# Group scores as the largest of ten pair sums, with new orders of work on all engines

## The chip, the cores and the metric

The kernel runs on one core of a Trainium2 chip. The metric is the device time of one execution in microseconds (us). Five engines work side by side, each through its own list of instructions in order, and wait for each other by semaphores: PE (TensorE, matrix products), DVE (VectorE), ACT (ScalarE), POOL (GpSimd) and SP (SyncE, which only starts DMAs here).

## The reference

The input is x, 2 batches x 1024 tokens x 128 channels in float32. A block of attention comes first, then a mixture of experts, each with a layer norm before and after and added to x:

```python
x = x + _layernorm(attn(_layernorm(x), W_basis, W_v, b_v, W_o, b_o))
x = x + _layernorm(ffn(_layernorm(x), gate_w, gate_bias, Wg, Wu, Wd, Sg, Su, Sd))

# attn: latent = x @ W_basis.T (R = 64); scores = latent @ latent.T / 8, causal softmax
# ffn: 64 experts of 88 hidden units, 2 shared ones; all experts are computed, rw weighs them
scores = sigmoid(x @ gate_w.T); choice = scores + gate_bias
group_scores = sum(top_k(choice.reshape(T, 8, 8), 2)[0], axis=-1)
_, gidx = top_k(group_scores, 4)          # 4 of 8 groups stay
_, idx = top_k(where(in_group, choice, 0), 8)
rw = 2.5 * scores[idx] / (sum(scores[idx]) + 1e-20)
routed = einsum('eth,te->th', expert_out, rw); out = routed + shared
```

The change touches one line of this, the sum of the two largest of each group of eight.

## The kernel before

The 2048 tokens are 16 tiles of 128, in four quads (q = 0 to 3) of four tiles; quads 0 and 1 are the first batch. The hidden units of the experts are cut into 11 rounds of 4 sets; a set is 128 hidden units, 8 of each of 16 experts. A step is one set (or shared expert part) with one quad of 512 tokens: gate and up products (six matmuls of 512 columns, since each float32 factor is split into a high and a low part and three products are taken), a SiLU on ACT, two products on DVE, the split of the hidden tile into high (ACT) and low (POOL), and the down product (three matmuls) into a PSUM bank that gathers the output of a quad.

Everything up to the end of round 0 is written out, step by step, by four lists of stages, `PE_ORDER`, `ACT_ORDER`, `DVE_ORDER` and `POOL_ORDER`; every engine runs its list in order and every stage holds its own waits. Rounds 1 to 9 follow in loops (`Fori`) that the change leaves alone. Round 10 and the output are written out again in `PE_TAIL`, `ACT_TAIL`, `DVE_TAIL` and `POOL_TAIL`.

A stage is a letter and a quad, with a tile number behind it for A, C, N and T. What the letters do:

- A: score rows of a tile (PE), row maximum (DVE L895), exponent (ACT L702). T: the exponents transposed by PE and copied by ACT (L712). C: weighing the values (PE L1258), squares and copy on ACT (L690, L693). D: the inverse root for the norm behind attention (POOL L539). U: adding attention to x (DVE L908). V, Q, P, S: values, latent, transposed norm and statistics of x.
- X: statistics of the new x on DVE (L864, L867), inverse root and shift on POOL (L523 to L530). Y: its norm on ACT (L672). E: transposed by PE (L1268), kept as x2_t and x_hi by ACT (L719, L720), x_lo by POOL (L512).
- F: logits (PE L1277), tanh (ACT L726), the sigmoid from it (DVE L925), the bias (POOL L587). H: group scores (DVE L935 to L945). J: choice of groups (DVE L953 to L960) and masking (POOL L596). I: choice of experts (DVE). O: their scores picked (DVE L976). M: the sum of weights (DVE L981 to L984) and the routes (POOL L575). G: the routes transposed (PE L1286), high part (ACT L734), low part (DVE L919). N: the routes spread over hidden units, two sets a stage (PE L1301, ACT L740).
- Z: gate and up of step q, on ACT the SiLU, on DVE the products (L1008, L1018, or L1080 for shared parts). Steps Z0 and Z1 are the shared parts of quad 0, Z2 to Z5 its four sets; Z6 to Z17 belong to quads 1 and 2, Z18 to Z23 to quad 3. W: hidden tile into high (ACT L768) and low (POOL L547); on PE, W of k is the down product of step k - 2. R: an expert set's weights split into high (ACT L748) and low (POOL L555). L: the same for the shared ones. B, K: small preparations.
- In the tail Z, W and R are as above, D is a down product, O the copy of a finished quad, T its centering on PE (L1457), S statistics, Y the inverse root on POOL, N the output.

Step Z with an odd number uses PSUM banks 2 and 3, which N uses too, so that Z3 waits for ACT's copies of N01. Route stages share bank 1 with F. H waits for the biased scores and sits in DVE's list like any other stage. These lines set two of the waits:

```python
if routed:
    pe.wait_ge(s_wlo, c + 1)          # first_gate_up: low weights of set c, stage R on POOL
pe.wait_ge(s_xlo, q + 1)
if s % 2 == 1:
    banks23_free(at)
...
def spread_route(q, h, at):           # stage N
    pe.wait_ge(s_rt, q + 1)           # low part of the routes, stage G on DVE
```

`link` gives an instruction an increment and waits for it, where the next pass reads what it wrote.

Of the kernel before, what the change touches and what calls it, by code (L numbers as in the profile page):

```python
# [51 lines left out]
def build(nc, x, w_basis_t, w_v, b_v, w_o_t, b_o, gate_w_t, gate_bias, w_experts, w_shared_up,  # L52
# [21 lines left out]
    with ExitStack() as ctx:  # L74
# [312 lines left out]
        def unit_bank(u):  # L387
# [1115 lines left out]
```

## Time and profile before

| | us |
|---|---|
| three runs | 480.24, 482.01, 482.15 |
| median | 482.01 |
| the profiled execution | 481.66 |
| its span, first to last instruction | 479.7 |
| mean granted clock of PE in the span | 0.992 |

The profile is of one execution. A page sums it up; behind it are views that group instructions by line, that list them in order of time (the timeline, with the idle time of the engine before each and what ended it), and that give the busy time of each engine in a window. All times are from the start of the span. The granted clock is 1.00 at 2.4 GHz and 0.50 at 1.2 GHz.

### The profile page before, as it was taken

The numbers are of one execution on the slowest core, as the hardware profiler recorded it, in microseconds if no ns is written. First come the engines' busy times: TensorE is split into PE (matmuls) and PEld (weight loads), VectorE is DVE, ScalarE is ACT, GpSimd is POOL, SyncE is SP. The second block draws the span as 40 slices with busy tenths as digits, with TensorE's granted clock in tenths as the row PEclk, the third lists the DMA queues.
The fourth block names the chain that finished last, engine by engine and source line by source line (L and its number), as shares of the span: only waits on it lengthen the run. The fifth ranks groups of instructions, "written<-read, shape, count | busy, mean of one in ns | idle before, by whom it ended". The sixth has DMA issues, their size and how long they took to land.

```text
span 479.7 us, 8058 instructions
## 1 busy us (share of the span) xinstructions
PE 454.6 (95%) x2152; PEld 370.0 (77%) x2152; DVE 326.3 (68%) x710; ACT 286.2 (60%) x573; POOL 335.5 (70%) x318
## 2 busy tenths in 40 slices
PE   6899876889999999999999999999999999999995
PEld 5788764667678888888888888888888888888884
DVE  5667879677566666666666666666666666666777
ACT  2688874765655655565555655555565555556554
POOL 6581845848577777767777777768776776778684
PEclk9999988999999999999999999999999999999999
DMA  7000100000011010100001010100001010100002
GB/s 182 21 3 1 33 2 8 27 1 0 1 34 35 16 34 16 34 16 20 29 16 33 16 33 16 33 16 20 30 16 33 16 33 16 32 1 0 0 24 66
DMA packets 12856, 11.58 MB, mean 24 GB/s; under 512 B 2549, under 2 KB 12837, under 8 KB 12837
## 3 DMA queue, kind: packets, MB, share of 16 engines
q1 hardware_dynamic: 11973, 11.02, 8.1%
q10 hardware_dynamic: 864, 0.33, 0.3%
q8 instruction: 9, 0.15, 0.1%
q14 instruction: 10, 0.08, 0.1%
HBM read 10.30 MB, written 1.05 MB: 24 GB/s over the span
## 4 chain that ended last, share of the span: by engine, by line
PE 84%; DVE 5%; POOL 4%; ACT 2%; issue 2%; DMA 1%; ACTq 0%; DVEq 0%; POOLq 0%
PE ps L1306 26%; PE ps L1308 26%; PE ps L1307 25%; PE ps L1258 2%; PE ps L1246 1%; PE ps L1457 1%; DVE neg_max L895 1%; PE ps L1301 1%; POOL xn L565 1%; POOL rstd L524 1%; DMA bv_sb<-in_b_v 1%; PE ps L1198 1%; DVE hid L1080 1%; POOL x_lo L512 1%; POOL w_lo L555 0%
## 5 line engine op out<-in xcount | busy, mean ns | idle before, releaser
L547 POOL TENSOR_TENSOR lat_hi<-hid,lat_hl 128x512 fp32r<-128x512 f32 (+1 forms) x187 | 240.5, 1288 | 96.7 <-ACT lat_hl L768 95.9
L754 ACT ACTIVATE ps<-ps 128x512 f32<-128x512 f32 (+1 forms) x180 | 103.0, 573 | 132.6 <-PE ps L1308 132.4
L1008 DVE TENSOR_TENSOR up_w<-ps,route_w 128x512 f32<-128x512 f32 (+1 forms) x180 | 122.1, 678 | 83.0 <-PE ps L1308 82.5
L1018 DVE TENSOR_TENSOR hid<-ps,up_w 128x512 f32<-128x512 f32 (+1 forms) x180 | 122.4, 680 | 36.5 <-DVE up_w L1008 28.3
L1306 PE MATMUL ps<-x_hi,w_hi 128*128 128x512 f32 (+1 forms) x360 | 141.0, 392 | 1.5 <-POOL w_lo L555 1.1
L1308 PE MATMUL ps<-x_hi,w_lo 128*128 128x512 f32 (+1 forms) x360 | 140.4, 390 | 0.0
L1307 PE MATMUL ps<-x_lo,w_hi 128*128 128x512 f32 (+1 forms) x360 | 140.1, 389 | 0.0
L768 ACT CAST lat_hl<-hid 128x512 fp32r<-128x512 f32 (+1 forms) x188 | 113.6, 605 | 17.8 <-DVE hid L1018 17.1
L1306 PEld LDWEIGHTS ps<-x_hi,w_hi 128*128 128x128 f32 x360 | 68.0, 189 | 18.1 <-POOL w_lo L555 1.5
L1308 PEld LDWEIGHTS ps<-x_hi,w_lo 128*128 128x128 f32 x360 | 67.9, 189 | 14.9
L1307 PEld LDWEIGHTS ps<-x_lo,w_hi 128*128 128x128 f32 x360 | 67.9, 189 | 14.5
L1306 PE MATMUL ps<-lat_hl,w_hi 128*128 128x512 f32 (+1 forms) x180 | 71.1, 395 | 0.0
L1308 PE MATMUL ps<-lat_hl,w_lo 128*128 128x512 f32 (+1 forms) x180 | 69.7, 387 | 0.0
L1307 PE MATMUL ps<-lat_hi,w_hi 128*128 128x512 f32 (+1 forms) x180 | 69.2, 385 | 0.0
L555 POOL TENSOR_TENSOR w_lo<-w_raw,w_hi 128x384 fp32r<-128x384 f32 x44 | 44.8, 1018 | 2.5 <-ACT w_hi L748 2.5
L1308 PEld LDWEIGHTS ps<-lat_hl,w_lo 128*128 128x128 f32 x180 | 33.7, 187 | 8.1
L1306 PEld LDWEIGHTS ps<-lat_hl,w_hi 128*128 128x128 f32 x180 | 33.8, 188 | 7.8 <-issue 0.7
L1307 PEld LDWEIGHTS ps<-lat_hi,w_hi 128*128 128x128 f32 x180 | 33.8, 188 | 7.3
L748 ACT CAST w_hi<-w_raw 128x384 fp32r<-128x384 f32 x44 | 22.8, 518 | 4.2 <-PE ps L1308 4.2
L1258 PE MATMUL ps<-vals,exp_t 128*128 128x129 f32 x144 | 19.5, 288 | 0.3 <-ACT att L693 0.2
L1258 PEld LDWEIGHTS ps<-vals,exp_t 128*128 128x128 f32 x144 | 18.3, 202 | 1.6 <-issue 1.5
L895 DVE TENSOR_REDUCE neg_max<-ps 128x1 f32<-128x128 f32 (+7 forms) x16 | 12.0, 753 | 9.6 <-PE ps L1228 9.5
(140 smaller groups left out, 363.2 us busy)
## 6 DMA issues: line engine op xcount, KB each, us to landing
w_raw<-in_w_experts SPq DMA_DIRECT2D x44, 192.0 KB, 2.3
x_sb<-in_x SPq DMA_DIRECT2D x3, 256.0 KB, 4.8
out<-x_sb SPq DMA_DIRECT2D x3, 256.0 KB, 2.3
x_sb<-in_x ACTq DMA_DIRECT2D x2, 64.0 KB, 2.3
x_sb<-in_x SPq DMA_DIRECT2D x2, 64.0 KB, 2.1
out<-x_sb SPq DMA_DIRECT2D x1, 128.0 KB, 1.8
out<-x_sb SPq DMA_DIRECT2D x2, 64.0 KB, 1.6
sh_raw<-in_w_shared_up SPq DMA_DIRECT2D x1, 88.0 KB
```

Source lines behind the costliest of these rows:

```text
L547: g.tensor_tensor(hid_lo[:, k % DEEP, 0:w], hid[:, k % 2, 0:w], hid_hi[:, k % DEEP, 0:w], ALU.subtract).then_inc(s_hlo, 1)
L555: g.tensor_tensor(w_lo[:, c, :], w_raw[:, c, :], w_hi[:, c, :], ALU.subtract).then_inc(s_wlo, 1)
L748: a.copy(w_hi[:, c, :], w_raw[:, c, :]).then_inc(s_whi, 1)
L754: a.activation(bank, bank, ACT.Silu).then_inc(s_gated, 1)
L768: a.copy(hid_hi[:, k % DEEP, 0:w], hid[:, k % 2, 0:w]).then_inc(s_hhi, 1)
L895: v.tensor_reduce(neg_max[:, k:k + 1], rows.rearrange("p a b -> p (a b)")[:, 0:width], AX.X, ALU.max, negate=True).then_inc(s_max, 1)
L1008: v.tensor_tensor(up_w[:, k % 2, 0:w], ps[:, gate_bank(k) + 1, 0:w], route_w[:, group, 512 * q + lo:512 * q + lo + w], ALU.mult).then_inc( ...
L1018: v.tensor_tensor(hid[:, k % 2, 0:w], ps[:, gate_bank(k), 0:w], up_w[:, k % 2, 0:w], ALU.mult).then_inc(s_hid, 1)
L1258: mm = t_.matmul(ps[:, 7, 256 * (r % 2):256 * (r % 2) + C + 1], exp_t[:, r % 2, j, :], vals[:, (q // QPB) * TPB + j, 0:C + 1], start=(j == 0),
L1306: t_.matmul(out_, hi, mhi, start=start, stop=False)
L1307: t_.matmul(out_, hi, mlo, start=False, stop=False)
L1308: return t_.matmul(out_, lo, mhi, start=False, stop=stop)
```

## The change

H on DVE takes seven passes instead of eleven. Before, it kept the largest and second largest of halves, quarters and eighths of a group in turn. Now it takes the larger and smaller of element k and k + 4 (four high and four low values) and forms ten sums: each high with its own low, and the six pairs of two high ones. The sum of the two largest of the group is the largest of these ten. The ten sums lie in a tile `pair_sum`, and one reduction over it gives the score.

The eight lists have the same stages as before in other orders. The first part of the diff declares the tiles; the lists are shown whole.

```diff
--- before.py
+++ after.py
@@ -131,9 +131,9 @@
 
         scores = sb("scores", [P, 2, 4, E])
         choice = sb("choice", [P, 2, 4, E])
-        big = [sb(f"big{n}", [P, 4 * GROUPS, 4 >> n]) for n in range(3)]
-        small = [sb(f"small{n}", [P, 4 * GROUPS, 4 >> n]) for n in range(3)]
-        low_big = sb("low_big", [P, 4 * GROUPS, 2])
+        high = sb("high", [P, 4 * GROUPS, 4])
+        low = sb("low", [P, 4 * GROUPS, 4])
+        pair_sum = sb("pair_sum", [P, 4 * GROUPS, 10])
         group_score = sb("group_score", [P, 4, GROUPS])
         group_find = sb("group_find", [P, 4, 8])
         group_left = sb("group_left", [P, 4, GROUPS])
@@ -260,33 +260,33 @@
             return [stage(name) for name in names.split()]
 
         PE_ORDER = stages(
-            "P0 Q0 K0 V0 P1 A00 A01 Q1 T00 T02 A02 A03 C00 C01 T04 T06 A10 A11 C02 C03 T10 A12 "
-            "T11 V1 T12 P2 A13 T13 Q2 C10 W0 C11 P3 T14 V2 T15 A20 Q3 T16 T17 C12 A21 C13 A22 "
-            "E0 V3 F0 T20 A23 T22 A30 T24 A31 C20 T26 C21 A32 W1 T30 T31 C22 C23 T32 T33 C30 "
-            "E1 A33 T34 F1 T35 C31 T36 T37 G0 Z0 C32 N00 E2 C33 Z1 F2 N01 G1 Z2 Z3 Z4 W2 W3 E3 "
-            "Z5 W4 Z6 N10 F3 W5 N11 G2 Z7 W6 W7 N20 Z8 Z9 W8 N21 Z10 Z11 W9 Z12 Z13 W10 W11 "
-            "W12 Z14 Z15 W13 G3 W14 Z16 N30 W15 W16 Z17 Z18 N31 W17 W18 Z19 Z20 W19 Z21 W20 "
+            "P0 Q0 K0 V0 A00 P1 A01 A02 Q1 T00 T02 A03 C00 C01 T04 T06 A10 C02 C03 A11 P2 V1 "
+            "T10 A12 T11 A13 W0 T12 Q2 T13 C10 C11 P3 T14 V2 T15 Q3 A20 T16 A21 T17 C12 C13 E0 "
+            "A22 A23 T20 F0 A30 T22 T24 V3 A31 T26 C20 C21 A32 C22 T30 T31 C23 T32 T33 C30 A33 "
+            "E1 T34 F1 T35 W1 C31 G0 T36 T37 Z0 C32 N00 C33 Z1 E2 F2 Z2 N01 G1 Z3 W2 Z4 W3 Z5 "
+            "E3 W4 Z6 N10 F3 N11 G2 W5 Z7 W6 W7 N20 Z8 Z9 W8 N21 Z10 Z11 W9 W10 Z12 W11 Z13 "
+            "W12 W13 Z14 Z15 G3 W14 Z16 N30 W15 W16 Z17 Z18 N31 W17 W18 Z19 Z20 W19 Z21 W20 "
             "Z22 W21 W22 Z23 "
         )
         ACT_ORDER = stages(
-            "P0 Q0 K0 P1 A00 A01 Q1 T00 T02 A02 A03 T04 C01 T06 A10 C03 T10 A11 T11 T12 P2 T13 "
-            "Q2 A12 C11 P3 A13 T14 T15 A20 L0 T16 T17 Q3 Y0 C13 A21 E0 F0 A22 T20 A23 T22 L1 "
-            "R0 A30 T24 T26 C21 R1 A31 T30 T31 C23 Y1 T32 T33 A32 E1 A33 T34 F1 T35 C31 T36 R2 "
-            "T37 G0 Z0 Y2 N00 E2 C33 Z1 R3 F2 W0 G1 N01 W1 Z2 W2 Z3 Z4 Y3 W3 E3 Z5 W4 W5 Z6 "
-            "N10 F3 N11 G2 W6 Z7 N20 W7 Z8 Z9 W8 N21 W9 Z10 Z11 Z12 W10 W11 Z13 W12 Z14 W13 "
-            "Z15 G3 W14 W15 Z16 N30 Z17 W16 W17 Z18 N31 Z19 W18 W19 Z20 W20 Z21 W21 Z22 R4 Z23 "
-            "W22 R5 "
+            "P0 Q0 K0 P1 A00 A01 Q1 T00 T02 A02 A03 T04 C01 T06 A10 C03 L0 A11 P2 T10 T11 T12 "
+            "T13 A12 Q2 C11 P3 A13 T14 T15 Q3 A20 T16 T17 Y0 C13 E0 A21 F0 A22 T20 T22 A23 A30 "
+            "T24 C21 R0 R1 T26 A31 T30 T31 C23 L1 T32 Y1 T33 A32 E1 T34 F1 A33 T35 C31 T36 G0 "
+            "R2 T37 Z0 N00 Y2 C33 Z1 E2 R3 F2 G1 W0 N01 W1 Z2 W2 Z3 Z4 Y3 W3 Z5 W4 E3 Z6 W5 "
+            "N10 F3 N11 W6 G2 Z7 N20 W7 Z8 Z9 W8 N21 Z10 W9 W10 Z11 Z12 W11 W12 Z13 W13 Z14 "
+            "Z15 G3 W14 Z16 N30 W15 W16 Z17 Z18 N31 W17 W18 Z19 W19 Z20 Z21 W20 W21 Z22 R4 W22 "
+            "Z23 R5 "
         )
         DVE_ORDER = stages(
-            "S0 B0 P0 S1 S2 B1 Q0 A00 A01 K0 V0 A02 A03 Q1 S3 A10 A11 A12 V1 U0 X0 Q2 A13 V2 "
-            "A20 A21 Q3 A22 U1 V3 F0 A23 A30 H0 X1 A31 J0 A32 I0 O0 M0 A33 U2 X2 F1 H1 G0 J1 "
-            "Z0 I1 O1 Z1 U3 F2 M1 H2 J2 X3 Z2 I2 G1 Z3 O2 Z4 Z5 M2 F3 Z6 G2 Z7 H3 Z8 Z9 J3 Z10 "
-            "Z11 I3 Z12 Z13 O3 M3 Z14 Z15 G3 Z16 Z17 Z18 Z19 Z20 Z21 Z22 Z23 "
+            "S0 B0 P0 S1 S2 B1 Q0 A00 A01 A02 K0 V0 A03 Q1 S3 A10 A11 A12 V1 U0 A13 Q2 X0 V2 "
+            "A20 A21 Q3 A22 A23 U1 F0 A30 X1 V3 H0 A31 A32 J0 I0 O0 M0 A33 U2 F1 X2 H1 G0 J1 "
+            "Z0 I1 O1 Z1 U3 F2 M1 H2 J2 X3 Z2 I2 Z3 G1 Z4 O2 Z5 M2 Z6 F3 G2 Z7 H3 Z8 Z9 J3 Z10 "
+            "I3 Z11 O3 Z12 M3 Z13 Z14 Z15 G3 Z16 Z17 Z18 Z19 Z20 Z21 Z22 Z23 "
         )
         POOL_ORDER = stages(
-            "S0 S1 P1 S2 P2 D0 S3 P3 B0 X0 D1 F0 X1 J0 L0 E0 D2 L1 R0 M0 R1 E1 F1 X2 J1 E2 D3 "
-            "F2 M1 J2 W0 R2 X3 W1 R3 W2 W3 W4 M2 F3 W5 W6 W7 W8 W9 J3 W10 W11 W12 M3 W13 W14 "
-            "W15 E3 W16 W17 W18 W19 W20 W21 R4 W22 R5 "
+            "S0 S1 P1 B0 S2 P2 D0 S3 P3 X0 D1 F0 X1 L0 J0 D2 E0 R0 M0 F1 R1 X2 E1 L1 J1 D3 E2 "
+            "F2 M1 W0 R2 J2 W1 X3 R3 W2 W3 W4 M2 F3 W5 W6 E3 W7 W8 J3 W9 W10 W11 W12 M3 W13 "
+            "W14 W15 W16 W17 W18 W19 W20 W21 R4 W22 R5 "
         )
         ROWS = [(q, r) for q in range(QUADS) for r in range(4)]
         TURNS = [(q, 2 * r + h) for q, r in ROWS for h in range(1 + (4 * (q % QPB) + r) // 4)]
@@ -388,22 +388,22 @@
             return (6, 7, 0, 7, 1)[u]
 
         PE_TAIL = stages(
-            "Z0 D0 Z1 D1 D2 Z2 D3 Z3 Z4 D4 Z5 D5 Z6 Z7 D6 D7 Z8 T0 Z9 D8 D9 Z10 D10 Z11 Z12 T1 "
-            "D11 Z13 D12 Z14 Z15 D13 D14 D15 Z16 Z17 D16 T2 D17 D18 Z18 Z19 T3 D19 D20 D21 D22 "
+            "Z0 D0 Z1 D1 D2 Z2 D3 Z3 Z4 D4 D5 Z5 D6 Z6 Z7 D7 Z8 T0 Z9 D8 Z10 D9 D10 Z11 Z12 T1 "
+            "D11 Z13 D12 Z14 D13 Z15 D14 Z16 D15 Z17 T2 D16 D17 D18 Z18 T3 Z19 D19 D20 D21 D22 "
             "T4 "
         )
         ACT_TAIL = stages(
-            "R2 W0 Z0 W1 Z1 R3 W2 Z2 W3 Z3 Z4 W4 W5 Z5 Z6 W6 W7 Z7 O0 Z8 W8 W9 Z9 Z10 W10 O1 "
-            "W11 Z11 Z12 W12 W13 Z13 Z14 Z15 W14 W15 W16 Z16 O2 Z17 W17 W18 Z18 Z19 O3 W19 W20 "
+            "W0 Z0 R2 Z1 W1 R3 W2 Z2 Z3 W3 Z4 W4 W5 Z5 Z6 W6 O0 Z7 W7 Z8 W8 W9 Z9 W10 Z10 O1 "
+            "W11 Z11 Z12 W12 W13 Z13 Z14 W14 Z15 O2 Z16 W15 W16 Z17 O3 W17 W18 Z18 Z19 W19 W20 "
             "Y4 P0 "
         )
         DVE_TAIL = stages(
-            "Z0 Z1 Z2 Z3 Z4 Z5 Z6 Z7 Z8 S0 Z9 Z10 Z11 Z12 S1 Z13 N0 Z14 Z15 N1 Z16 Z17 S2 Z18 "
+            "Z0 Z1 Z2 Z3 Z4 Z5 Z6 Z7 Z8 S0 Z9 Z10 N0 Z11 Z12 S1 Z13 Z14 Z15 N1 Z16 Z17 S2 Z18 "
             "Z19 W20 S3 O4 N2 S4 N3 N4 "
         )
         POOL_TAIL = stages(
-            "W0 R2 W1 R3 W2 W3 W4 W5 W6 W7 W8 Y0 W9 W10 W11 W12 W13 Y1 W14 W15 W16 W17 W18 Y2 "
-            "W19 Y3 "
+            "W0 R2 W1 R3 W2 W3 W4 W5 W6 W7 W8 W9 Y0 W10 W11 W12 W13 Y1 W14 W15 W16 W17 W18 W19 "
+            "Y2 Y3 "
         )
 
         def acc_bank(q):
@@ -932,18 +932,15 @@
                     dve.wait_ge(s_gin, q)
 
                 grp = choice[:, k].rearrange("p t (g k) -> p (t g) k", k=GE)
-                tt(big[0][:], grp[:, :, 0:4], grp[:, :, 4:8], ALU.max)
-                link(tt(small[0][:], grp[:, :, 0:4], grp[:, :, 4:8], ALU.min))
-                for n in range(2):
-                    w = 2 >> n
-                    b0, b1 = big[n][:, :, 0:w], big[n][:, :, w:2 * w]
-                    tt(big[n + 1][:], b0, b1, ALU.max)
-                    tt(low_big[:, :, 0:w], b0, b1, ALU.min)
-                    link(tt(small[n + 1][:], small[n][:, :, 0:w], small[n][:, :, w:2 * w],
-                            ALU.max))
-                    link(tt(small[n + 1][:], small[n + 1][:], low_big[:, :, 0:w], ALU.max))
-                link(tt(group_score[:, :, :].rearrange("p t g -> p (t g)"), big[2][:, :, 0],
-                        small[2][:, :, 0], ALU.add))
+                tt(high[:], grp[:, :, 0:4], grp[:, :, 4:8], ALU.max)
+                link(tt(low[:], grp[:, :, 0:4], grp[:, :, 4:8], ALU.min))
+                tt(pair_sum[:, :, 0:4], high[:], low[:], ALU.add)
+                tt(pair_sum[:, :, 4:7], high[:, :, 0:3], high[:, :, 1:4], ALU.add)
+                tt(pair_sum[:, :, 7:9], high[:, :, 0:2], high[:, :, 2:4], ALU.add)
+                link(tt(pair_sum[:, :, 9:10], high[:, :, 0:1], high[:, :, 3:4], ALU.add))
+                link(v.tensor_reduce(group_score[:, :, :].rearrange("p t g -> p (t g)"),
+                                     pair_sum[:], AX.X, ALU.max))
+
             def choose_groups(q):
 
                 if q:
```

## Rows read from the trace of the kernel before

**Rows 1.** Busy time of each engine over the whole span, from the page

```profile
PE 454.6 (95%) x2152; PEld 370.0 (77%) x2152; DVE 326.3 (68%) x710; ACT 286.2 (60%) x573; POOL 335.5 (70%) x318
```

**Rows 2.** Windows: length, busy PE, PEld, DVE, ACT, POOL; granted clock, DMA

```profile
178.00:435.00 257.00, 257.00 (x1114) 208.66 (x1113) 171.13 (x248) 149.50 (x279) 190.57 (x155) 1.00 0.08 23
...
31.00:60.00 29.00, 26.63 (x205) 23.75 (x204) 21.01 (x71) 25.16 (x72) 16.47 (x23) 1.00 0.05 15
60.00:88.30 28.30, 19.75 (x93) 15.69 (x92) 23.07 (x112) 17.40 (x38) 15.86 (x21) 0.88 0.05 13
88.30:135.00 46.70, 43.92 (x188) 32.31 (x187) 30.30 (x80) 29.07 (x54) 30.23 (x26) 1.00 0.01 2
66.00:70.00 4.00, 3.71 (x21) 3.58 (x21) 3.85 (x23) 2.33 (x5) 1.84 (x2) 0.58 0.00 2
76.00:80.00 4.00, 3.85 (x12) 3.27 (x13) 3.65 (x28) 2.57 (x5) 0.66 (x2) 0.57 0.00 0
```

**Rows 3.** Timeline, PE after its waits: start us, us, what, [idle before, releaser]

```profile
13.77 0.63 PE L1162 MATMUL ps<-ident,xn 128*128 128x128 f32 x4 [1.02 <-POOL xn L565]
...
53.51 0.66 PE L1268 MATMUL ps<-ident,xn 128*128 128x128 f32 x4 [0.84 <-ACT exp_t L712]
...
65.44 0.73 PE L1301 MATMUL ps<-route_t,sel 128*128 128x512 f32 x2 [2.58 <-issue]
...
76.14 1.05 PE L1286 MATMUL ps<-ident,route 128*128 128x128 f32 x4 [2.71 <-POOL route L575]
```

**Rows 4.** Timeline of DVE from 60 to 65 us

```profile
60.14 0.87 DVE L864 BATCH_NORM_STATS2 stats<-x_sb 128x6 f32<-128x128 f32 x4
...
61.34 0.26 DVE L925 TENSOR_SCALAR scores<-scores 128x256 f32<-128x256 f32 x1
62.44 0.29 DVE L935 TENSOR_TENSOR big<-choice 128x128 f32<-128x128 f32 x1 [0.84 <-POOL choice L587]
62.65 0.28 DVE L936 TENSOR_TENSOR small<-choice 128x128 f32<-128x128 f32 x1
...
64.41 0.19 DVE L945 TENSOR_TENSOR group_score<-big,small 128x32 f32<-128x32 f32 x1
64.64 0.69 DVE L919 TENSOR_TENSOR route_t<-ps,route_t 64x512 fp32r<-64x512 f32 x1
```

**Rows 5.** DVE reductions by form, 0 to 130 us: busy us, mean ns, idle

```profile
L981 DVE TENSOR_REDUCE wsum<-left 128x4 f32<-128x256 f32 x4 | 1.7, 414 | 0.1
...
L895 DVE TENSOR_REDUCE neg_max<-ps 128x1 f32<-128x384 f32 x2 | 1.1, 558 | 1.1 <-PE ps L1228 1.1
```

**Rows 6.** Timelines of DVE and POOL: the same passes alone and beside POOL

```profile
41.21 1.14 DVE L908 SCALAR_TENSOR_TENSOR x_sb<-att,rstd,x_sb 128x128 f32<-128x128 f32 x4 [1.14 <-POOL rstd L539]
...
56.34 3.77 DVE L908 SCALAR_TENSOR_TENSOR x_sb<-att,rstd,x_sb 128x128 f32<-128x128 f32 x4
...
74.96 1.04 POOL L575 TENSOR_TENSOR route<-left,winv 128x512 f32<-128x512 f32 x1 [0.32 <-DVE winv L984]
...
74.99 1.16 DVE L936 TENSOR_TENSOR small<-choice 128x128 f32<-128x128 f32 x1
```

**Rows 7.** Costs on POOL (page, then timeline) and on ACT (timeline)

```profile
L547 POOL TENSOR_TENSOR lat_hi<-hid,lat_hl 128x512 fp32r<-128x512 f32 (+1 forms) x187 | 240.5, 1288 | 96.7 <-ACT lat_hl L768 95.9
...
L555 POOL TENSOR_TENSOR w_lo<-w_raw,w_hi 128x384 fp32r<-128x384 f32 x44 | 44.8, 1018 | 2.5 <-ACT w_hi L748 2.5
...
62.49 0.33 POOL L523 TENSOR_SCALAR var_e<-mv 128x4 f32<-128x4 f32 x1
...
64.37 0.20 POOL L530 TENSOR_TENSOR shift<-var_e,rstd 128x4 f32<-128x4 f32 x1
...
77.71 1.08 ACT L740 COPY route_w<-ps 128x512 f32<-128x512 f32 x2
```

**Rows 8.** Timelines of PE and POOL near the end

```profile
471.92 0.71 PE L1457 MATMUL ps<-center,y_t 128*128 128x128 f32 x4 [0.61 <-ACT y_t L843]
...
471.05 1.04 POOL L524 TENSOR_TENSOR rstd<-var_e,minus_half 128x4 f32<-128x4 f32 x1
```

## The prediction

> **What bounds the kernel now.** I read the page first, then windows by stage, then the timelines of the engines. TensorE is busy for 95% of the span [rows 1], but the share is an average over three stages. In the loop over the rounds it has no idle time: 257 of 257 us, 1114 matmuls, so 0.231 us each [rows 2]. Nothing in the diff touches that loop, and no faster route can shorten it. From 31 to 60 us (the attention of the second half) PE is idle for 29.0 - 26.6 = 2.4 us, from 60 to 88.3 us (routing beside the first experts) for 28.3 - 19.75 = 8.55 us, and from 88.3 to 135 us for 2.8 us [rows 2]. This idle time, some 14 us, is all that a new order can win on the way to the loop. To it comes a clock effect in the middle stage: the granted clock means 0.58 from 66 to 70 us and 0.57 from 76 to 80, which is the lower level, 1.2 GHz, for most of both. Each fall stands right behind a long pause of PE, of 2.58 and of 2.71 us [rows 3]. Their cost is 3.71 x 0.42 + 3.85 x 0.43 = 3.2 us [rows 2].
>
> The two pauses name the chain. The first, ahead of N00 at 65.44 us, is put down to issue; but N00 needs the low part of the routes, which DVE finishes at 64.64 + 0.69 = 65.33 us [rows 4]. DVE had it behind X2 (60.14), F1 (61.34), a wait of 0.84 for the biased scores from POOL, and H1, the group scoring itself, 62.44 to 64.64 [rows 4]. The second pause, ahead of G1 at 76.14, ends when POOL has written the routes of quad 1 [rows 3]. So the bound from 60 to 88 us is a loop of DVE, POOL and ACT in turn, with PE at its end.
>
> **The change, part by part.** *The scoring.* Before, H takes 2.20 us from its first pass to the next stage. An unlinked 128x128 pass holds DVE for 0.21 us, the last linked pass, of 32 elements, for 0.23 [rows 4]. The new passes are 128 and 128 elements (0.21, and 0.32 with its link), then 128, 96, 64 and 32 (0.21, 0.18, 0.14, 0.23), then a reduction of 320 elements. No row shows that reduction; between 256 elements at 414 ns and 384 at 558 [rows 5] it is 0.41 to 0.56, and I take 0.48, with a link 0.52. The sum is 1.81, so 0.4 us less for each of four H: 1.6 us of DVE. Only H1 and H2 lie where DVE is waited for. If runs of ten elements were slow and the reduction took twice that, H would be as long as before and the forecast 0.8 us worse.
>
> *The start.* A00 goes ahead of P1 and fills the 1.02 us wait of PE for xn at 13.77 [rows 3] with three short matmuls: -0.35 us.
>
> *The rows, 31 to 60 us.* A33 moves ahead of E1, where PE waited 0.84 us for exp_t behind Y1 on ACT [rows 3]; A22 and A23 move ahead of T20 and F0. R0, R1 and L1 on ACT now stand directly ahead of copies that PE needs (about 0.5 us each for R), so part comes back. Walked queue by queue, small waits of 0.2 to 0.4 us stay at C30, E1 and T34 and the 2.4 us become 1.4: -1.0. From both ends: all 2.4 go, or 1 is added.
>
> *N00.* On DVE F1 goes ahead of X2, on POOL F1 ahead of R1 and E1. POOL now stands in F1 until DVE has passed U2. Queued behind it are R1, X2, E1, L1 and J1; DVE waits for X2's result through ACT, and J1. But this leaves U2 alone on DVE: its four passes took 3.77 us at 56.34 beside a busy POOL and 1.14 alone at 41.21 [rows 6]. F1 comes at about 55.5, POOL adds the bias during X2 (the 0.84 wait is covered), H1 runs from about 57 and G0 ends near 60, while PE reaches N00 only near 61: the pause of 2.58 goes. What is late next is ACT: its queue (Z0's gate with the table load, N00's copies, Y2, C33's square, Z1, then E2's copy) delivers x2_t some 1.2 us after PE wants it for F2. The exchange of E2 and C33 on PE hides only E2.
>
> *G1, Z3, Z5.* Z2 now stands ahead of N01 and G1, so six matmuls (1.39 us) cover the route chain (F2, M1 on DVE, M1 on POOL); I get 0.85 us of wait at G1 for the 2.71 before. The cover is spent: behind G1 comes Z3, which needs both copies of N01, and on ACT these stand behind G1's copy and W0. That is four copies of 0.54 [rows 7], 2.2 us of new wait. Then Z5 needs R3, on POOL behind W0, R2, J2, W1, X3: after G1 two copies on ACT (1.1), then 1.29 + 1.02 + 0.65 + 1.29 + 2.1 (62.49 to 64.57) + 1.02 = 7.35 [rows 7], 8.45 in all; PE has G1, the wait, Z3, W2, Z4, W3 = 0.4 + 2.2 + 18 x 0.231 = 6.75, so it waits 1.7 to 1.9. With 0.15 at Z4 the stage holds 1.2 + 0.85 + 2.2 + 0.15 + 1.9 = 6.3 us instead of 8.55: -2.25.
>
> *The clock.* Two falls followed pauses of 2.6 and 2.7 us; the pauses now are 2.2 and 1.9 at most. I keep one fall of the two: -1.6, with 0 and -3.2 as ends.
>
> *DVE beside POOL.* H1 now runs while POOL works through R1 and X2. A 0.28 us pass of H2 took 1.16 us when POOL's route pass had begun 0.03 us before it [rows 6], so +0.9 for one such collision; I take +0.6, since G0 ends about 1 us before PE wants it. The Trainium skill (SBUF — State Buffer, "Who interferes with whom") says that a VectorE instruction with two SBUF inputs and a GpSimd instruction that reads SBUF lock each other out, and that tensor_reduce never does. By that rule, with which the 1.16 us agrees, six of the seven new passes can still be blocked, one for as long as a POOL instruction lasts.
>
> *88.3 to 135 us.* The waits at Z7, N20 and N21 shrink with a shorter H3 and an earlier G2; I3 and O3 now stand ahead of Z11 and Z12 on DVE, which gives some back: 2.8 becomes 2.1, -0.7 (ends -2 and +1).
>
> *The tail.* T3 moves ahead of Z19 and O3 on ACT ahead of W17 and W18. That removes the 0.61 us wait at 471.92 [rows 8] but holds back Z19, on whose hidden tile D22 waits; Y2 on POOL (1.04 us at 471.05 for its second step [rows 8]) goes behind W19 and delays N2. Sum +0.3, ends -0.4 and +0.8.
>
> The sum: -0.35 - 1.0 - 2.25 - 1.6 + 0.6 - 0.7 + 0.3 = -5.0 us. The profiled execution took 481.66 us (span 479.7), so 476.7; it lies 0.35 below the median of the three runs, 482.01, so I say 477.0.
>
> **The rivals.** *More is won, 474.* If the clock does not fall at all (-1.6) and the waits at Z3 and Z5 are half of my walk (about -2), 477.0 becomes 473.4 to 474. For it: PE is never idle as long as before either fall. Against it: the pauses stand close together.
>
> *The wait moves, 480.3.* The chain behind G1 ends no earlier because something before it slips, and the freed pauses come back at F2, Z3 and Z5: 2 us more of waits than my 6.3 and both falls of the clock (+1.6) leave 477.0 + 3.6 = 480.6, and 480.3 with the start better filled. For it: the new cover order has Z3 and Z5 exposed. Against it: N00's pause goes by two independent reasons.
>
> *Slower, 484.5.* DVE and POOL now start their two-input passes at the same time more often. If H1, O1 and H2 are stretched as U2 was, by (3.77 - 1.14) / 4 = 0.66 us a pass [rows 6], six passes each in H1 and H2 and one in O1 add 8.6 us to the chain of G1 and Z5, less some 1 us of slack at N00. That puts 477.0 at 484.5. It decides from about 5 us of stretch on, where the gain is gone. Against it: POOL's queue has gaps of its own there, and three of the four H before ran at full speed. The Trainium skill's rule above is what would cause it.
>
> *The change does not do what it says,* H as long as before: 477.8, inside the first range.
>
> **How the numbers follow.** Forecast 477.0 (its own range 474.5 to 479.5) 0.57; more is won 0.18; the wait moves 0.18; slower 0.07. The range for 8 in 10 takes in most of the second and third case and stops short of the fourth: 473.3 to 481.2. A measurement of this kernel can tell about 0.5%, 2.4 us, from no change, so faster means under 479.6: 0.57 x 0.98 + 0.18 = 0.74; slower over 484.4: 0.05; the same: 0.21.
>
> **What would show it.** Right: the loop's window still without idle time; no pause of over 1 us ahead of N00; the four passes of U2 near 1.1 us; H at 1.8 us; PE ready for Z3 before ACT has N01's copies; at most one stretch at the lower clock. Wrong: idle time from 31 to 60 us above 2.4 us, so that ACT bounds the rows; passes of H1 or H2 stretched beside POOL; a pause at Z5 of over 3 us; or waits inside the loop, which would say that the order leaves a mark there.

## The result, and the profile after

The changed kernel took 476.53 us (median of four runs, 475.69 to 477.60) beside 481.22 for four runs of the kernel before, a ratio of 0.9886 with the interval 0.9864 to 0.9909. Over the later comparisons the kernel before had medians of 482.01 to 482.16, so the gain is 4.7 to 5.5 us. The forecast was 477.0. The profiled execution of the changed kernel is its slowest of the four: 477.60 us, span 475.6. Behind H, line numbers are three lower than before.

The busy time of the engines, from the page, beside [rows 1]; then the windows of [rows 2], with a window at the start and one around the low clock:

```profile
PE 455.8 (96%) x2152; PEld 370.5 (78%) x2152; DVE 325.5 (68%) x694; ACT 286.0 (60%) x573; POOL 335.9 (71%) x318
```

```profile
135.00:435.00 300.00, 300.00 (x1299) 243.47 (x1299) 199.86 (x289) 175.01 (x327) 224.07 (x183) 1.00 0.08 23
31.00:60.00 29.00, 27.73 (x214) 24.84 (x214) 22.29 (x87) 25.46 (x72) 12.91 (x18) 1.00 0.03 8
60.00:88.30 28.30, 22.47 (x114) 17.60 (x112) 25.19 (x100) 20.28 (x45) 20.30 (x26) 0.88 0.08 22
88.30:135.00 46.70, 44.80 (x191) 33.17 (x190) 30.05 (x73) 29.18 (x55) 30.37 (x26) 1.00 0.02 5
9.00:18.00 9.00, 8.27 (x31) 6.18 (x32) 4.84 (x18) 2.89 (x7) 8.37 (x12) 0.62 0.36 103
74.00:81.00 7.00, 4.78 (x11) 3.80 (x12) 6.67 (x38) 4.08 (x8) 5.61 (x7) 0.51 0.11 30
```

The loop is as before: 300 us without idle time, 0.231 us a matmul. Idle time fell from 2.37 to 1.27 us from 31 to 60 us, from 8.55 to 5.83 from 60 to 88.3, and from 2.78 to 1.90 up to 135. The matmul counts of the windows rose because more of the work is done by then. Around the middle one stretch at the low clock is left, 74 to 81 us, but it is as long as the two of before together: the mean from 60 to 88.3 us is 0.88 in both kernels.

The row of 9 to 18 us is new: clock 0.62, where the same window of the kernel before has 1.00:

```profile
9.00:18.00 9.00, 6.85 (x38) 5.05 (x39) 5.86 (x19) 4.46 (x12) 8.62 (x12) 1.00 0.36 103
```

The fall begins at about 9 us, ahead of anything that the change moves. Stage V2 begins at 33.28 us instead of 31.84, so this execution lost 1.44 us by then, and the changed kernel profiled again below (e9_after_again) did nearly the same. Seven of the fourteen executions profiled in this study have a clock of 0.62 to 0.81 in that window, two of them with the old start (e1_passes, e3_f1first), so it is not peculiar to the change; in five of the seven the fall comes at about 14 us. Stages are compared from V2 on.

PE after its waits, beside [rows 3] and [rows 8]:

```profile
68.55 1.08 PE L1274 MATMUL ps<-gw_sb,x_t 128*128 128x64 f32 x8 [1.38 <-ACT x_t L719]
...
73.23 0.63 PE L1283 MATMUL ps<-ident,route 128*128 128x128 f32 x4 [1.70 <-POOL route L575]
...
76.22 0.77 PE L1303 MATMUL ps<-x_hi,w_hi 128*128 128x512 f32 x1 [2.37 <-ACT route_w L740]
...
97.49 0.70 PE L1298 MATMUL ps<-route_t,sel 128*128 128x512 f32 x2 [1.05 <-DVE hid L1077]
...
468.87 0.39 PE L1303 MATMUL ps<-lat_hl,w_hi 128*128 128x256 f32 x1 [0.49 <-POOL lat_hi L547]
```

The pause ahead of N00 is gone (it begins at 63.12), and on DVE two stages of the chain to it, U2 and G0, are short and early:

```profile
57.02 1.13 DVE L908 SCALAR_TENSOR_TENSOR x_sb<-att,rstd,x_sb 128x128 f32<-128x128 f32 x4
...
61.78 0.69 DVE L919 TENSOR_TENSOR route_t<-ps,route_t 64x512 fp32r<-64x512 f32 x1
```

On PE no wait over 0.3 us stands ahead of Z4 or Z5. F2, G1 and Z3 wait 1.38, 1.70 and 2.37. At N21 the wait is what it was (1.06 before). In the tail the 0.61 ahead of T3 is gone and 0.49 ahead of D19 has come.

The gain by stages, from the starts of PE's stages in the traces (us; e4_front is the changed kernel with the old tail, below):

| from, to | before | after | e4_front |
|---|---|---|---|
| V2 to N00 | 33.60 | 29.84 | 29.84 |
| N00 to G1 | 10.70 | 10.11 | 10.12 |
| G1 to N21 | 25.04 | 24.26 | 23.99 |
| N21 to T4 | 373.37 | 372.96 | 372.61 |
| V2 to T4 | 442.71 | 437.17 | 436.56 |

Two thirds of the 5.54 us lie ahead of N00. One trace of a kernel is not exact to the last digit: from F2 to F3 the changed kernel took 19.22 us here and 18.83 when it was profiled again.

### The profile page after: what moved, and what is told of

It reads as the page before. It is cut to its first block, busy times and chain, and to the rows that moved or that the text cites. A ratio compares the mean times of both kernels' runs of the same rounds, so it can differ in the third digit from the quotient of the medians.

```text
span 475.6 us, 8043 instructions
## 1 busy us (share of the span) xinstructions
PE 455.8 (96%) x2152; PEld 370.5 (78%) x2152; DVE 325.5 (68%) x694; ACT 286.0 (60%) x573; POOL 335.9 (71%) x318
## 3 DMA queue, kind: packets, MB, share of 16 engines
HBM read 10.30 MB, written 1.05 MB: 24 GB/s over the span
## 4 chain that ended last, share of the span: by engine, by line
PE 89%; ACT 5%; DVE 2%; issue 2%; DMA 1%; ACTq 0%; POOL 0%; DVEq 0%
PE ps L1303 27%; PE ps L1305 26%; PE ps L1304 26%; PE ps L1255 2%; PE ps L1243 1%; PE ps L1203 1%; PE ps L1274 1%; PE ps L1298 1%; PE ps L1195 1%; PE ps L1223 1%; PE ps L1224 1%; PE ps L1454 1%; DMA bv_sb<-in_b_v 1%; ACT xn L672 1%; ACT exp_t L712 1%
## 5 line engine op out<-in xcount | busy, mean ns | idle before, releaser
L1255 PE MATMUL ps<-vals,exp_t 128*128 128x129 f32 x144 | 18.3, 278 | 0.6 <-ACT att L693 0.4
L1255 PEld LDWEIGHTS ps<-vals,exp_t 128*128 128x128 f32 x144 | 17.1, 191 | 1.4 <-issue 1.2
```

The source lines that it names most:

```text
L1255: mm = t_.matmul(ps[:, 7, 256 * (r % 2):256 * (r % 2) + C + 1], exp_t[:, r % 2, j, :], vals[:, (q // QPB) * TPB + j, 0:C + 1], start=(j == 0),
```

## The experiments

Ratios are to the kernel before, with their 95% intervals. All kernels compute the whole of the reference.

### One half of the change at a time

**e1_passes**: the seven passes, every list as before. **e2_orders**: the lists of the changed kernel, the eleven passes.

> The seven passes alone, all eight lists as before. Theory (the orders carry the gain; shorter passes move only the two places where DVE is waited for): G0 comes 0.4 us earlier, so the 2.58 us pause ahead of N00 shrinks to about 2.2, H2 shortens J2 and with it the later waits by up to 0.4, in all -0.4 to -0.8 us against the kernel before. Rival (the scoring is the bound of the whole stage from 60 to 88 us, all of the gain comes from it): -4 us or more. Rival (the seven passes are not quicker): 0, with H at 2.2 us in the timeline.

> All eight new lists, but the eleven passes of before in H. Theory: keeps the gain but for 0.4 to 1.0 us, so -3.7 to -4.5 us against the kernel before. Rival (orders and passes need each other, since the new cover fits only the shorter H): the gain falls to -2 us or less.

e1_passes: 481.72 us, ratio 0.9978 (0.9958 to 0.9997), some 1.1 us faster by the ratio, but the medians differ by only 0.3. Its trace has the pause ahead of N00 at 1.94 instead of 2.58, and V2 to N00 0.77 us shorter (32.83); 2.2 and 0.4 were expected. From V2 to T4 this execution won nothing (442.96), with a clock of 0.76 from 60 to 88.3 us.

e2_orders: 479.63 us, 0.9948 (0.9929 to 0.9966), 2.5 us faster. Apart the halves bring 3.6 us by the ratios, together 5.5; each value is known to about 1 us, so the two sums lie only just apart. The forecast of e2_orders (3.7 to 4.5) missed by over 1 us. The rival, that the halves need each other, put it at 2 us or less; the measured 2.5 lies nearer to it.

From V2 to T4 the trace of e2_orders has 440.42 us, 3.25 more than the changed kernel. Of this 0.78 stand ahead of N00 (30.62 against 29.84): the longer H0 delays the row maxima and PE waits 0.58 us for exp_t at 50.54, and G0 ends only 0.11 us ahead of N00. F2, G1 and Z3 wait as they do after. The greater part stands at N21, where neither theory had it. First its PE, then DVE and POOL during H3:

```profile
98.05 1.19 PE L1301 MATMUL ps<-route_t,sel 128*128 128x512 f32 x2 [2.53 <-DVE hid L1080]
```

```profile
92.02 1.38 DVE L936 TENSOR_TENSOR small<-choice 128x128 f32<-128x128 f32 x1
...
94.23 1.34 DVE L940 TENSOR_TENSOR big<-big 128x32 f32<-128x32 f32 x1
...
91.90 1.36 POOL L512 TENSOR_TENSOR x_lo<-x_t,x_hi 128x512 fp32r<-128x512 f32 x1
...
94.22 1.30 POOL L547 TENSOR_TENSOR lat_hi<-hid,lat_hl 128x512 fp32r<-128x512 f32 x1 [0.96 <-ACT lat_hl L768]
```

Two passes of H3 are held up, each by the POOL instruction that began 0.01 to 0.12 us before it, and each for as long as that lasts. The pass of 32 elements takes 1.34 us instead of 0.19. The changed kernel at the same place:

```profile
92.94 1.38 DVE L936 TENSOR_TENSOR low<-choice 128x128 f32<-128x128 f32 x1
...
95.11 0.49 DVE L941 TENSOR_REDUCE group_score<-pair_sum 128x32 f32<-128x320 f32 x1
...
92.80 1.37 POOL L512 TENSOR_TENSOR x_lo<-x_t,x_hi 128x512 fp32r<-128x512 f32 x1
...
95.14 1.30 POOL L547 TENSOR_TENSOR lat_hi<-hid,lat_hl 128x512 fp32r<-128x512 f32 x1 [0.97 <-ACT lat_hl L768]
```

When POOL's second instruction comes, DVE is in the reduction, which takes 0.49 us beside it and 0.48 alone (H0). H3 lasts from 92.74 to 95.60, 2.86 us, against 4.40 in e2_orders (91.82 to 96.22), and the wait at N21 is 1.05 against 2.53: the 1.5 us of H3 pass to PE whole. Behind it the clock falls (98.05: 1.19 us for what took 0.70; the granted clock is 0.62 from 98 to 102 us, 1.00 in the changed kernel), and N21 to T4 is 374.37 us, 1.4 over the changed kernel. So 1.5 and 1.4 at N21 and 0.8 ahead of N00 make the difference, less 0.4 in small amounts between. The 0.49 us of the reduction agrees with the rule of the Trainium skill (SBUF — State Buffer, "Who interferes with whom") that the prediction named, by which a reduction is never held up.

### F1 ahead of X2, alone

**e3_f1first**: the kernel before, with this in the lists of DVE and POOL:

```diff
-A33 U2 X2 F1 H1 G0
+A33 U2 F1 X2 H1 G0
-R0 M0 R1 E1 F1 X2 J1
+R0 M0 F1 R1 E1 X2 J1
```

> The kernel before with one edit on two engines: on DVE F1 ahead of X2, on POOL F1 ahead of R1 and E1. Theory (POOL standing in F1 leaves U2 alone on DVE, and POOL's bias is covered by X2): the four passes of U2 fall from 3.77 to about 1.14 us, the pause ahead of N00 goes from 2.58 us to under 0.8, and 2 to 3.5 us are won against the kernel before, as the next pause, ahead of G1, moves earlier along with it. Rival (the pause ahead of G1 is set by its own chain and takes up what N00 gives): the pause ahead of G1 grows from 2.71 to over 4 us and under 1 us is won. Rival (delay of R1, E1 and X2 on POOL costs more): slower than before.

481.24 us, ratio 0.9979 (0.9961 to 0.9997): 1.0 us faster, where 2 to 3.5 was forecast. U2 lasts 1.57 instead of 3.77 [rows 6], but the wait at N00 is still 1.53 (2.58 before; under 0.8 was forecast), because H1 now takes 3.8 us instead of 2.2. Two of its passes stand beside POOL's R1 and x_lo:

```profile
61.43 0.83 DVE L935 TENSOR_TENSOR big<-choice 128x128 f32<-128x128 f32 x1
62.18 1.37 DVE L936 TENSOR_TENSOR small<-choice 128x128 f32<-128x128 f32 x1
...
62.06 1.34 POOL L512 TENSOR_TENSOR x_lo<-x_t,x_hi 128x512 fp32r<-128x512 f32 x1
```

The changed kernel has X2 ahead of E1 on POOL, and x_lo comes behind H1 (62.26). G1 still waits 2.71. So this exchange alone brings 1.05 of the 3.76 us ahead of N00. All the new orders with the old passes (e2_orders) bring 2.98 of them, and the passes the other 0.78.

### The old tail

**e4_front**: the changed kernel with the four tail lists of before.

> The changed kernel with the four tail lists of before. My forecast gave the new tail +0.3 us, so this would be 0.3 us faster than the changed kernel. The two profiles say the reverse: from N31 to T4 the changed kernel gained 0.1 us more. Either way within 0.5 us of the changed kernel, -4.2 to -5.2 us against before. Rival (the tail carries a real part): under -3.7 us.

475.59 us, ratio 0.9862 (0.9833 to 0.9891). The 0.61 us wait at T3 is back, and yet N21 to T4 is 0.35 us shorter than with the new tail (372.61 against 372.96; the six other kernels whose lists from N21 on are those of the changed kernel have 372.94 to 373.00). e11_e3late and e12_reorder (below), whose lists from N21 on differ only in the tail, say the same: 373.99 with the new tail, 373.70 with the old. The new tail costs 0.3 us, as forecast; by the times alone, whose intervals overlap, it could not be told.

### Z2 back behind G1

**e5_z2back**, in PE's list:

```diff
-E2 F2 Z2 N01 G1 Z3
+E2 F2 N01 G1 Z2 Z3
```

> The changed kernel with one edit on PE: Z2 back behind G1 (F2 N01 G1 Z2 Z3). Theory (Z2 covers the same 1.4 us of waiting on either side, so its move turned a wait at G1 into one at Z3): the wait ahead of G1 grows from 1.70 to about 3.1 us, the wait ahead of Z3 falls from 2.37 to about 1.0, and the time stays within 1 us of the changed kernel. Rival (the move is what won the time from 60 to 88 us): slower by 1.5 us or more than the changed kernel, since Z2's hidden tile comes later and Z4 waits for it.

476.31 us, ratio 0.9875 (0.985 to 0.99), the same as with Z2 early. G1 waits 3.05, Z3 not at all, and Z5 0.66 for w_lo. From F2 to F3 PE takes 19.03 us, against 19.22 after and 18.96 in e4_front. The forecast had 1.0 at Z3 and nothing at Z5. The 1.4 us of cover only choose between the waits; the end is set elsewhere.

### ACT's copies of N01 early

**e6_n01early**, in ACT's list:

```diff
-F2 G1 W0 N01 W1 Z2
+F2 W0 N01 G1 W1 Z2
```

> The changed kernel with one edit on ACT: F2 W0 N01 G1 W1 in place of F2 G1 W0 N01 W1. ACT stands from 70.05 to 73.89 us in G1, with N01's products ready in PSUM from about 71.5. Theory (the 2.37 us wait ahead of Z3 is this order on ACT and nothing else): the wait ahead of Z3 goes to under 0.3, and since W0 on POOL starts 3 us sooner too, nothing later takes its place at once; PE is not idle for 4 us in a stretch of 6 any more, so the fall of the clock behind it (74 to 81 us) may go too: 2 to 4 us faster than the changed kernel. Rival (Z5, behind R3 on POOL, takes up the time): under 1 us faster, with a new wait ahead of Z5 or Z4.

479.74 us, ratio 0.9939 (0.9916 to 0.9961): some 3 us slower than the changed kernel, where 2 to 4 us faster was forecast. The wait at Z3 shrank to 0.40, as the theory said, and a longer one came at Z4. PE, then DVE and POOL during H2:

```profile
73.40 0.47 PE L1303 MATMUL ps<-x_hi,w_hi 128*128 128x512 f32 x1 [0.40 <-ACT route_w L740]
...
79.53 0.77 PE L1303 MATMUL ps<-x_hi,w_hi 128*128 128x512 f32 x1 [3.81 <-DVE hid L1015]
```

```profile
71.22 1.16 DVE L936 TENSOR_TENSOR low<-choice 128x128 f32<-128x128 f32 x1
72.41 1.25 DVE L937 TENSOR_TENSOR pair_sum<-high,low 128x128 f32<-128x128 f32 x1
73.58 1.10 DVE L938 TENSOR_TENSOR pair_sum<-high 128x96 f32<-128x96 f32 x1
...
71.19 1.04 POOL L575 TENSOR_TENSOR route<-left,winv 128x512 f32<-128x512 f32 x1 [0.32 <-DVE winv L981]
72.18 1.32 POOL L547 TENSOR_TENSOR lat_hi<-hid,lat_hl 128x512 fp32r<-128x512 f32 x1
73.47 1.06 POOL L555 TENSOR_TENSOR w_lo<-w_raw,w_hi 128x384 fp32r<-128x384 f32 x1
```

With W0 early on ACT, POOL has W0 and R2 ready right behind the routes and never pauses, so three passes of H2 are held up in a row, where the changed kernel has one (1.16 at 72.08) and an idle POOL of 1.99 us behind it. H2 takes 4.42 us against 2.63, and DVE's Z2, behind H2, J2 and X3, ends 11.67 us after F2 (79.38), against 10.36 in the changed kernel. There PE comes for Z4 11.65 us after F2 and does not wait; here it is ready 8.0 us after F2 and waits until 11.82. So the most that the edit could have won at Z4 is 1.3 us, and the held passes took that. The loss comes behind it: after 3.81 us of waiting PE runs at 1.2 GHz until 88.3 us:

```profile
79.50:88.30 8.80, 8.77 (x21) 6.21 (x22) 7.09 (x21) 5.31 (x12) 5.98 (x7) 0.50 0.08 24
```

F2 to F3 is 22.85 us instead of 19.22. This is the mechanism of the rival "slower", met outside the change.

### Keeping the clock up

**e7_filler**: short matmuls, overwritten later, in the two waits of PE: 6 at G1, 8 at Z3.

```diff
@@ route_high, PE @@
+if q == 1:
+    for _ in range(6):
+        t_.matmul(ps[:, 1, 0:P], ident[:], ident[:], start=True, stop=True)
@@ first_gate_up, PE @@
+if s == 3:
+    pe.wait_ge(s_xhi, 3)
+    for _ in range(8):
+        t_.matmul(ps[:, 0, 0:P], ident[:], ident[:], start=True, stop=True)
```

> The changed kernel with 6 extra 128-column products on PE while it waits for G1 and 8 while it waits for Z3, into banks that nobody reads then; their results are overwritten. This prices the lower clock alone. Theory (the low clock from 74 to 81 us costs PE about 1.6 to 2 us and follows from PE standing idle): the clock stays at 1.00 through that stretch and the kernel is 1.5 to 2 us faster than the changed one. Rival (the time there is bound by ACT, DVE and POOL, and a faster PE only waits longer): the clock stays up and the time changes by under 0.5 us.

477.11 us, ratio 0.9886 (0.9863 to 0.991): nothing won in the whole. Two things meet in it. The first six matmuls were in the way: PE ran F2 to N01 at the low clock in this execution, reached them late and began G1 1.2 us after POOL's routes were done (71.53; it is 0.15 us in the changed kernel), so that F2 to G1 took 5.74 us instead of 4.68:

```profile
70.49 1.04 POOL L575 TENSOR_TENSOR route<-left,winv 128x512 f32<-128x512 f32 x1 [0.32 <-DVE winv L981]
...
72.75 0.60 PE L1286 MATMUL ps<-ident,route 128*128 128x128 f32 x4
```

Behind Z3 the clock did stay at 2.4 GHz, and most of the time came back as a wait at Z5:

```profile
81.72 0.50 PE L1306 MATMUL ps<-x_hi,w_hi 128*128 128x512 f32 x1 [1.59 <-POOL w_lo L555]
```

POOL's chain W0, R2, J2, W1, X3, R3 ends at 82.19 us in the changed kernel (w_lo, 81.17 and 1.02), 8.96 us after G1. PE at 1.2 GHz reaches Z5 at 82.92, 0.7 us behind it; at 2.4 GHz it is there 1.6 us early and waits. So the low clock and the chain to R3 lie side by side, and only what the clock adds behind the end of the chain is paid. G1 to Z5 takes 8.97 us here and 9.69 at the low clock; G1 to F3 takes 13.90, against 14.54 in the changed kernel and 14.15 when it was profiled again. So the clock is worth 0.3 to 0.7 us, and not the 1.5 to 2 of the forecast.

### H of quad 1 twice

**e8_h_twice**: `for _ in range(2 if q == 1 else 1):` around the seven passes.

> The changed kernel with the group scoring of quad 1 run twice (+1.8 us on DVE ahead of G0). PE reaches N00 0.65 us after G0 is done. Theory (H1 has just that slack, so in the changed kernel it is nearly on the path): N00 is 1.2 us late, the wait ahead of F2 shrinks by what ACT had queued anyway, and the time grows by 0.5 to 1.2 us. Rival (H1 is still the bound): +1.8 us or more. Rival (H1 is covered): under +0.3 us.

479.81 us, ratio 0.9939 (0.9918 to 0.9961): some 3 us more than the changed kernel for 1.8 us of added work (from V2 to T4 the trace has 439.29 us, 2.1 more). The forecast was 0.5 to 1.2; the rival, 1.8 or more, held. The second scoring runs into POOL's x_lo (`62.63 1.39 DVE L938`, POOL's 1.26 us from 62.61) and lasts 3.4 us, from 62.07 to 65.46; N00 waits 2.66 us. In the changed kernel G0 ends at 62.47 and N00 begins at 63.12, so the scoring of quad 1 has 0.65 us to spare and what is beyond that reaches PE. Its end is what brings a pause ahead of N00 back.

### Attempts at a better kernel, with the changed kernel beside them

**e9_after_again** is the changed kernel. **e10_r2gap_filler** has R2 on POOL ahead of D3, in a gap, and the 8 short matmuls at Z3 alone. **e11_e3late** has E3 on POOL back behind W15. **e12_reorder** goes further:

```diff
@@ e10: POOL @@
-L1 J1 D3 E2 F2 M1 W0 R2 J2
+L1 J1 R2 D3 E2 F2 M1 W0 J2
@@ e11: POOL @@
-W5 W6 E3 W7
+W5 W6 W7
-W14 W15 W16
+W14 W15 E3 W16
@@ e12: as e10 and e11 on POOL without the matmuls, old tail, and @@
-POOL W0 J2 W1 X3 R3 W2
+POOL W0 W1 R3 J2 X3 W2
-ACT  F2 G1 W0 N01 W1 Z2 W2 Z3 Z4 Y3 W3
+ACT  F2 W0 Z2 N01 G1 W1 W2 Z3 Z4 W3 Y3
-DVE  H2 J2 X3 Z2 I2 Z3
+DVE  H2 Z2 J2 X3 Z3 I2
-PE   Z5 E3 W4
+PE   Z5 W4 E3
```

> The changed kernel once more, unaltered, on the chip of the other three, so that they are compared with it and not only with the kernel before. Expected: 5 to 6 us faster than the kernel before, and a profile with the same waits (1.4 ahead of F2, 1.7 ahead of G1, 2.4 ahead of Z3, 1.05 ahead of N21).

> The changed kernel with R2 on POOL moved up into the 2.4 us in which POOL waits for D3, and 8 extra products on PE in its wait for Z3 alone, behind G1, so that they delay nothing that the route needs (6 extra products ahead of G1 had delayed it by 1 us). Theory (from 74 to 83 us two chains end together at Z5: PE at the lower clock, and POOL's W0 R2 J2 W1 X3 R3; each alone wins nothing, both together do): Z5 starts about 1 us sooner and 0.8 to 1.5 us are won against the changed kernel. Rival (a third chain, DVE's Z2 and Z3, holds Z4 or Z5): under 0.5 us.

> The changed kernel with one edit: E3 on POOL back to where it stood before the change, behind W15. In the changed kernel E3 begins at 92.80 us and the second pass of H3 at 92.94 takes 1.38 us for 0.28. Theory (DVE's passes with both inputs in SBUF stand while a POOL instruction runs): without E3 there the pass takes 0.28 us, H3 1.85 instead of 2.95, the wait ahead of N21 falls from 1.05 us to under 0.2, and 0.8 to 1.3 us are won. Rival (the stretch has another cause, or N21 waits for the gate on ACT): the pass or the wait stays, and under 0.4 us is won.

> An order made from what the profiles showed: the tails of before; on ACT Z2 and N01 ahead of G1, W3 ahead of Y3; on DVE Z2 ahead of J2 and Z3 behind X3; on POOL R2 in the wait for D3, W1 and R3 ahead of J2, E3 behind W15; on PE E3 behind W4. Theory (Z3, Z4 and Z5 were held by the order of short steps on ACT and POOL, not by the route itself): the waits ahead of Z3 and N21 go, Z5 starts 2 us sooner, and 2.5 to 4.5 us are won against the changed kernel. Rival (the locks between DVE and POOL come back when POOL runs W0, W1 and R3 beside H2, as they did with W0 and R2): H2 takes over 4 us, Z4 waits for it, and it is no faster than the changed kernel.

| | us | ratio | F2 to F3 | N21 to T4 |
|---|---|---|---|---|
| e9_after_again | 476.73 | 0.9903 (0.9866 to 0.994) | 18.83 | 372.97 |
| e10_r2gap_filler | 475.34 | 0.9861 (0.9829 to 0.9892) | 17.91 | 372.94 |
| e11_e3late | 477.35 | 0.9915 (0.9886 to 0.9945) | 18.98 | 373.99 |
| e12_reorder | 477.35 | 0.9904 (0.9868 to 0.9939) | 18.59 | 373.70 |

e10_r2gap_filler is the fastest by its median, 1.4 us under e9_after_again; the intervals overlap, and the traces show 0.9 us of it: V2 to F2 takes 35.2 us in both, and what differs is F2 to F3, 17.91 us where the changed kernel had 18.83 and 19.22. The clock is 1.00 all the way from 60 to 88.3 us. PE now waits for DVE's Z2 and Z3 at Z4 and Z5, 0.66 and 0.46 us, and no more for R3:

```profile
79.58 0.47 PE L1303 MATMUL ps<-x_hi,w_hi 128*128 128x512 f32 x1 [0.66 <-DVE hid L1015]
```

The 1.59 us wait of e7_filler suggests that both parts are needed, since a shorter POOL chain is worth something only when PE's clock is up. Neither part was run alone, so this is not shown.

e11_e3late shows that H3's blocked pass cost nothing in the changed kernel. Its DVE at H3 and Z6, and its PE at Z18:

```profile
91.22 0.28 DVE L936 TENSOR_TENSOR low<-choice 128x128 f32<-128x128 f32 x1
...
94.03 0.69 DVE L1077 TENSOR_TENSOR hid<-gated,ps 128x512 f32<-128x512 f32 x1 [1.24 <-ACT gated L762]
```

```profile
116.15 0.47 PE L1303 MATMUL ps<-x_hi,sh_hi 128*128 128x512 f32 x1 [1.33 <-issue]
```

The pass is back at 0.28 us, H3 ends 1.1 us sooner, and DVE then waits 1.24 for ACT; N21 waits 1.05 as ever. The forecast, 0.8 to 1.3 us won, failed with that. In exchange x_lo of quad 3 ends at 116.05 (114.78 and 1.27), and Z18, which needs it, begins at 116.15 after 1.33 us of idle time (put down to issue in the row), as in e12_reorder (1.35). So E3's early place is worth 1.0 us (373.99 against 372.97), and its collision fits into a slack of about 1.1 us, which e2_orders overruns with a second blocked pass.

e12_reorder has W0 on POOL right behind the routes again, and H2 has two blocked passes (1.16 at 72.20, 1.28 at 73.39) and lasts 3.6 us; Z4 and Z5 wait 1.18 and 1.41 and the clock falls at 82. These exchanges, each with a reason of its own, brought 0.2 us from F2 to F3, less than the two traces of the changed kernel differ by, where 2.5 or more was expected; the rival, that the held passes come back, had it right.

## Why the prediction was right

The total was right, 477.0 for 476.5, with the sign and, ahead of N00, the mechanism. Its terms were so far off in single places, in both directions, that the total owes something to luck. By stages, from the start of V2 on, the forecast's terms and the traces (us):

| won | forecast | measured |
|---|---|---|
| V2 to N00: rows 1.0, pause 2.58, less 0.6 | 2.98 | 3.76 |
| N00 to F3: waits 2.25 less the pause's 2.58, clock 1.6 | 1.27 | 0.75 |
| F3 to T4: 0.7, tail -0.3 | 0.4 | 1.03 |
| sum | 4.65 | 5.54 |

- *Start, -0.35: not so.* Where the clock at the start is as before, V2 begins at 31.80 to 32.02 us in five kernels with the new start (e6_n01early: 32.44), against 31.84 before. In the five the wait ahead of P1 shrinks from 1.02 to between 0.20 and 0.47, and nothing comes of it. What the start does do is vary from execution to execution: with the low clock V2 comes 1.3 to 2.0 us later (3.2 in e1_passes), which the forecast did not know.
- *Rows, 2.4 to 1.4: right,* 1.27 by the window.
- *N00: right,* by the reasons given. U2 took 1.13 us in place of 3.77, and G0 behind H1 ended 0.65 us ahead of N00. V2 to N00 gained 3.76, near the sum of the rows' 1.0 and the pause's 2.58.
- *H, 1.81 us: right where it is alone.* H0 took 1.76 us (46.44 to 48.20), its reduction 0.48. "Only H1 and H2 lie where DVE is waited for" failed: by e2_orders H0 counts too (0.58 at 50.54), and above all H3, at N21, where the eleven passes with the new lists cost 1.5 us and the clock 1.4 more.
- *F2 1.2, Z3 2.2: right,* 1.38 and 2.37. *G1 0.85: twice that,* 1.70. Of the difference 0.55 stands in one row: the sigmoid of F2 took 0.83 us instead of 0.28, beside POOL's x_lo:

```profile
70.08 0.83 DVE L925 TENSOR_SCALAR scores<-scores 128x256 f32<-128x256 f32 x1 [0.47 <-ACT scores L726]
...
69.03 1.73 POOL L512 TENSOR_TENSOR x_lo<-x_t,x_hi 128x512 fp32r<-128x512 f32 x1 [0.69 <-ACT x_hi L720]
```

  The routes stand behind it. The walk counted its chain at undisturbed durations.
- *Z5 1.7 to 1.9: none,* and *the clock, one fall kept: right in number, wrong in worth.* The chain on POOL was well sized, 8.96 us after G1 against 8.45. But the low clock at Z3 delays PE just while that chain runs, and the one stretch is as long as the two of before: counted as in the prediction it makes PE's own work 4.78 x 0.49 = 2.3 us longer, against 3.2 before, so 0.9 us less and not 1.6. By the forecast's terms G1 to Z5 takes 6.75, 1.9 for the wait and 1.6 for the clock, 10.25 us; it took 9.69, because the two costs overlap (e7_filler). The 0.6 us made up for most of G1's 0.85.
- *DVE beside POOL, +0.6: the collision came, the cost did not.* A pass of H1 took 0.81 us instead of 0.28, but G0 still ended 0.65 us ahead of N00. H2 and H3 had one each (1.16 and 1.38), and the one of H3 stayed within its slack (e11_e3late). The one that reached PE was the sigmoid's 0.55 at G1, which no term stood for.
- *88.3 to 135, 2.1: right,* 1.90. *Tail, +0.3: right,* 0.35 by e4_front. With it the stretch from N21 to T4 still became 0.41 us shorter, so 0.76 were won there apart from the tail. No term stood for that, and no run shows where it comes from.

Rival "slower" did not come: U2 stands alone on DVE, and POOL has 1.99 us of idle time during H2 where H's passes fit. e6_n01early took the second away and met the rival's mechanism, at 3 us and not 7.5: the blocked passes only ate the gain, and the low clock behind the wait made the loss.

Open: why the clock falls at 9 or 14 us in some executions and not in others. In the two that fell at 9 us PE had waited 0.99 and 0.94 us ahead of P0, against 0.23 before, but e6_n01early waited 0.91 there and kept its clock. Open too is whether the remaining 0.3 of G1 has a place of its own.

## What to carry to other kernels

Before giving a helper engine its work earlier, look at what DVE does at that moment: an idle POOL beside a row of short two-input passes can be worth more than the copy it would start. Where POOL can't be kept idle, a reduction in place of the last short passes may help: here it took 0.49 us beside POOL and 0.48 alone. A low clock and a wait for another engine's chain overlap when they run side by side; price the later end of the two, and expect a gain only from a change that shortens both. Split a reordering from the arithmetic it comes with, since one may be worth much less without the other, as the new orders were here.

## What the runs showed that was not expected

- A one-input pass is held up too: TENSOR_SCALAR on 128x256 took 0.83 us instead of 0.28 beside POOL's x_lo. In e6_n01early, e7_filler and e8_h_twice, where it met x_lo later in its course, it took 0.36, 0.58 and 0.57, and in all four it ended 0.15 us after x_lo. (x_lo itself took 1.73 us instead of 1.27, but that is not the sigmoid's doing: it began beside the last passes of U3, and took 1.71 in e6_n01early too.) The Trainium skill (SBUF — State Buffer, "Who interferes with whom") lists tensor_scalar among the operations that can contend; the prediction had left that out.
- The length of a blocked pass did not follow its size: 32 elements took 1.34 us and 128 took 1.38, each as long as the POOL instruction (1.30 and 1.36) that began just before. The 0.81 of H1 fits in: POOL's R1 (59.11, 1.00) was a third over when the pass began at 59.46. These passes, and the three of e6_n01early, ended 0.05 to 0.16 us after the POOL instruction, so the cost is what is left of it.
- From N21 to T4, 373 us, the same lists repeat within 0.06 us (372.94 to 373.00 over seven kernels with that part unchanged), so 0.3 us can be told there in a single trace, where the time of the whole changed kernel spreads over 2 to 3 us.
